# A decoder layer on one core: the attention stage takes rows transposed by the host, GpSimd adds the exponentials of the two key tiles, and the query halves are summed in turn

## The chip, the cores and the metric

The kernel runs on one core of a Trainium2 chip. The metric is the device time of one execution in microseconds; 687.07 us is the median of three runs (686.49 to 687.9).

## What is computed

One layer of a decoder on x of 8 batches x 256 rows x 512: attention, a long convolution against a context, and a feed-forward block with ternary weights. The change touches the attention alone:

```python
def rmsnorm(x):
    return x * jax.lax.rsqrt(jnp.mean(x * x, axis=-1, keepdims=True) + EPS)
x_ = _layernorm(x, axis=-1)
Q = (x_ @ Wq).reshape(B, T, HQ, Dh).transpose(0, 2, 1, 3)     # B 8, T 256, HQ 16, Dh 32
V = (x_ @ Wv).reshape(B, T, HKV, Dh).transpose(0, 2, 1, 3)    # HKV 4
Q = rmsnorm(Q)
K = rmsnorm(V)
scores = jnp.einsum('bhgtd,bhsd->bhgts', Q.reshape(B, HKV, g, T, Dh), K)
p = jax.nn.softmax(scores, axis=-1)                           # the mask is empty
y = jnp.einsum('bhgts,bhsd->bhgtd', p, V)
x = x + rmsnorm(y @ Wo)
```

A layer norm of the new x follows, whose rows are the queries of the convolution.

## The kernel before

The program is a sequence of stages. The attention stage takes the batches one at a time: a **turn** i of 8 does the scores, exponentials, sums, values and output projection of batch i, and between them the projections Q and V of batch i+1, and the transposed rows (xn2) of batch i-1 for the convolution. Turns 1 to 5 are a loop, turns 0, 6 and 7 are written out; turn 0 makes no projections (batch 1's are made ahead of it) and turn 7 has no next batch. Every engine has its own list of instructions, written by hand in `turn` of its block, and runs it in that order; semaphores alone tie the engines together. So a wait in one list holds everything behind it on that engine.

In a turn TensorE (PE) makes 16 scores tiles (`scores(i, n)`, L246): key head kv (of 4), key tile s (of 2, 128 keys each) and query half gp (of 2, 512 columns each). They go alternately to the two PSUM banks SB, ScalarE (ACT) takes each by `exponential` (L396) into `pt`, and score n waits for exponential n-2. Between the scores stand `x_transpose` (L205, the normalised rows of batch i+1, copied out by ACT's `x_out`, L360), `v` (L211) and `q` (L217). Then `sum_weights` (L264) multiplies all of `pt` by ones for the softmax sums, `q2_transpose` (L254) turns the rows of batch i-1, `sum_values` (L273) makes p V, `qk_transpose` (L229, L233) turns Q and K of the next batch, and `project` (L284) multiplies by Wo. A matmul in f32 shows as two records in the trace.

VectorE (DVE) has `rows_in` (statistics and normalised rows of batch i+2), `qk_norms` (the root of the mean squares of batch i+1 by Newton steps), `q_normalise` (L528), for each query half a reciprocal of the sums (L550) and a product (L555), `q_low` (L543: the low parts of Q), and `residual` (L560 on). After `q_low`, the SyncE queue (SP) issues 16 DMAs that spread Q over the partitions (`spread_q`, L158: 4 to each key head, semaphores d_qx0 to d_qx3). ACT also sums the feed-forward weights (`weight_sums`, L417: two tiles of 128x2048 in each turn). GpSimd (POOL) has only the powers of 128x2 variances (L639) and a copy of V (L646).

These lines set the order of the scores and what they wait for, before:

```python
def score(n):
    return n // 4, n // 2 % 2, n % 2        # kv, s, gp
...
if n % 4 == 0:
    wait(pe, d_qx[kv], i, 4 * 16)
...
if n >= 2:
    wait(pe, s_e, i, n - 1)
```

## Time and profile before

| | us |
|---|---|
| median of 3 runs | 687.07 |
| the profiled execution, its own time | 686.38 |
| its span in the trace | 684.6 |
| a turn of the loop, first score to first score | 32.3 |
| turns 1 to 6 together (63.20 to 256.87) | 193.67 |
| turn 0 (31.69 to 63.20) | 31.51 |
| turn 7 (256.87 to 286.66) | 29.79 |

The span is what the trace covers; the execution's own time is 1.8 us more. The attention stage ends with turn 7 at about 287 us; the convolution and the feed-forward block follow. Times in the rows below are microseconds from the start of the span unless marked ns.

### The profile page before, as it was taken

The numbers are of one execution on the slowest core, as the hardware profiler recorded it, in microseconds if no ns is written. First come the engines' busy times: TensorE is split into PE (matmuls) and PEld (weight loads), VectorE is DVE, ScalarE is ACT, GpSimd is POOL, SyncE is SP. The second block draws the span as 40 slices with busy tenths as digits, with TensorE's granted clock in tenths as the row PEclk, the third lists the DMA queues.
The fourth block names the chain that finished last, engine by engine and source line by source line (L and its number), as shares of the span: only waits on it lengthen the run. The fifth ranks groups of instructions, "written<-read, shape, count | busy, mean of one in ns | idle before, by whom it ended". The sixth has DMA issues, their size and how long they took to land.

```text
span 684.6 us, 10990 instructions
## 1 busy us (share of the span) xinstructions
PE 624.9 (91%) x3074; PEld 355.3 (52%) x3074; DVE 508.5 (74%) x981; ACT 455.5 (67%) x799; POOL 269.7 (39%) x248
## 2 busy tenths in 40 slices
PE   5889999999999998989999999948799999999995
PEld 3535454545454543467777777723344444444442
DVE  3556757575847373547887788789999999999983
ACT  2354666676665746168889888845876777577691
POOL 1000010001010003057777777624665666566572
PEclk9969999999999997999999999978999999999999
DMA  8564153627180816045666556511011100100001
GB/s 316 140 182 93 31 124 123 148 97 191 55 240 17 234 37 153 11 145 162 168 192 173 173 164 193 156 70 31 17 32 48 45 31 31 61 31 31 31 17 46
DMA packets 42309, 72.51 MB, mean 106 GB/s; under 512 B 4720, under 2 KB 16496, under 8 KB 42160
## 3 DMA queue, kind: packets, MB, share of 16 engines
q1 hardware_dynamic: 42288, 72.26, 36.7%
q8 instruction: 10, 0.16, 0.1%
q14 instruction: 11, 0.09, 0.0%
HBM read 47.51 MB, written 4.28 MB: 76 GB/s over the span
## 4 chain that ended last, share of the span: by engine, by line
PE 26%; DVE 24%; issue 5%; DVEq 1%; ACT 1%; POOL 0%; ACTq 0%; POOLq 0%
PE ps L708 20%; DVE toep L1189 4%; DVE xq L1175 3%; PE ps L1066 3%; DVE mb L1193 3%; DVE act8t L1225 2%; PE ps L1054 2%; DVE mx L1160 1%; DVE x_all L1138 1%; DVE st L1143 1%; DVE xn L1156 1%; DVE qo L761 1%; DVEq L69 1%; DVE ot L1233 1%; DVE cx L1171 0%
## 5 line engine op out<-in xcount | busy, mean ns | idle before, releaser
L708 PE MATMUL ps<-kv,toep 128*128 128x288 f32 x640 | 157.1, 409 | 1.1 <-PEq L1378 1.1
L708 PEld LDWEIGHTS ps<-kv,toep 128*128 128x128 f32 x640 | 122.2, 191 | 36.0 <-issue 2.2
L1066 PE MATMUL ps<-wt,xqt 128*128 128x512 bf16 x512 | 123.8, 387 | 9.4 <-DVE toep L1189 8.5
L1318 POOL TENSOR_TENSOR big<-toep,wst 128x512 f32<-128x512 f32 x64 | 83.6, 1306 | 59.7 <-DVE toep L1189 59.7
L396 ACT ACTIVATE big<-ps,kscale 128x512 f32<-128x512 f32 x128 | 84.3, 695 | 14.1 <-PE ps L246 13.3
L246 PE MATMUL ps<-qx,kx 128*128 128x512 f32 x128 | 76.7, 634 | 12.4 <-ACT big L396 12.1
L1066 PEld LDWEIGHTS ps<-wt,xqt 128*128 128x128 bf16 x512 | 48.3, 99 | 67.1 <-DVE toep L1189 11.9
L761 DVE TENSOR_REDUCE qo<-big 128x2048 f32 (+1 forms) x32 | 72.2, 2257 | 0.0
L1104 ACT ACTIVATE asq<-toep 128x512 f32<-128x512 f32 x64 | 39.5, 618 | 44.7 <-DVE sm L1199 43.7
L696 POOL TENSOR_TENSOR kv<-ctx 128x768 f32<-128x768 f32 (+1 forms) x32 | 52.5, 1642 | 37.0 <-PE ps L708 28.2
L750 DVE TENSOR_TENSOR big<-ps,qd 128x1024 f32<-128x1024 f32 x32 | 39.2, 1225 | 37.0 <-ACT ys L840 34.4
L1054 PE MATMUL ps<-wt,act8t 128*128 128x512 bf16 x256 | 59.9, 379 | 7.3 <-DVE act8t L1225 7.3
L550 DVE RECIPROCAL yt<-ps 128x512 f32<-128x512 f32 x16 | 53.6, 3351 | 14.6 <-PE ps L264 14.6
L217 PE MATMUL ps<-wq_s,xt 128*128 128x512 f32 x128 | 63.3, 593 | 0.8 <-ACT xt L360 0.8
L800 POOL TENSOR_TENSOR big<-ys,qd 128x768 f32<-128x768 f32 x32 | 56.3, 1759 | 13.7 <-ACT ys L840 11.5
L284 PE MATMUL ps<-wo_s,yt 128*128 128x512 f32 x128 | 56.6, 594 | 1.0 <-DVE yt L555 1.0
L246 PEld LDWEIGHTS ps<-qx,kx 128*128 128x128 f32 x128 | 25.7, 205 | 46.4 <-ACT big L396 26.6
L646 POOL COPY vo<-vn 128x256 f32<-128x256 f32 x8 | 3.2, 397 | 111.7 <-PE ps L273 86.3
L1189 DVE TENSOR_TENSOR toep<-ps,kv 128x512 f32<-128x512 f32 x64 | 43.5, 680 | 3.8 <-ACT kv L1095 2.4
L1054 PEld LDWEIGHTS ps<-wt,act8t 128*128 128x128 bf16 x256 | 23.9, 98 | 40.4 <-DVE act8t L1225 11.0
L1093 ACT ACTIVATE kv<-ps 128x512 f32<-128x512 f32 x64 | 37.6, 587 | 10.6 <-PE ps L1066 10.6
L1193 DVE TENSOR_REDUCE mb<-big 128x1 f32<-128x512 f32 x64 | 43.3, 677 | 0.0
(121 smaller groups left out, 1018.5 us busy)
## 6 DMA issues: line engine op xcount, KB each, us to landing
qx<-kv SPq DMA_DIRECT2D x128, 128.0 KB, 2.4
wst<-in_wall SPq DMA_DIRECT2D x12, 1024.0 KB, 6.8
wst<-in_wall SPq DMA_DIRECT2D x48, 256.0 KB, 3.8
toep<-krows SPq DMA_DIRECT2D x32, 256.0 KB, 3.7
ctx<-in_ctxt SPq DMA_DIRECT2D x32, 192.0 KB, 2.6
out_y<-ot SPq DMA_DIRECT2D x16, 256.0 KB, 2.0
conv_part<-qo SPq DMA_DIRECT2D x14, 256.0 KB, 2.7
x_all<-in_x SPq DMA_DIRECT2D x2, 1536.0 KB, 14.4
```

The source lines that it names most:

```text
L217: mm = pe.matmul(bank[:, t, :], xt[:, k, t * P:(t + 1) * P], wq_s[:, k, :], start=(k == 0), stop=(k == CK - 1))
L246: pe.matmul(SB[:, n % 2, :], kx[:, kv, s * P:(s + 1) * P].bitcast(F32R), qx[:, kv, gp * C:(gp + 1) * C].bitcast(F32R), start=True, stop=Tr ...
L284: mm = pe.matmul(OB[:, t, :], yt[:, k, t * P:(t + 1) * P], wo_s[:, k, :], start=(k == 0), stop=(k == CK - 1))
L396: act.activation(pt[:, s, kv, gp * C:(gp + 1) * C], SB[:, n % 2, :], ACT.Exp, scale=kscale[:, c:c + 1]).then_inc(s_e.sem, 1)
L708: mm = pe.matmul(m.ps[:, LB * r + lb, :].rearrange("p (b s) -> p b s", s=WIDE)[:, :, 0:PAIRS], m.toep[r][:, d * P:(d + 1) * P], m.kv[r][:, ...
L761: nc.vector.tensor_reduce(qo[:, :, bass.ds(h * HD, HD)], z[r][:], AX.X, ALU.add).then_inc(s_red.sem, 1)
L800: nc.gpsimd.tensor_tensor(z[r][:, :, :, HD - SHIFTS:HD].rearrange("p n j s -> p n s j"), window(ys[r][:], SHIFTS - 1, (SHIFTS * EW, NB), ( ...
L1054: mm = pe.matmul(DB, act8t[:, k, :], down_w[:, k, :], start=(k == 0), stop=(k == FK - 1))
L1066: mm = pe.matmul(bank[:, n % 2, :], xqt[r][:, k, :], wt[:, k, n * C:(n + 1) * C], start=(k == 0), stop=(k == CK - 1))
L1189: nc.vector.tensor_tensor(a[n % 2][:], UB[:, n % 2, :], r2[n % 2][:], ALU.mult).then_inc(s_a.sem, 1)
L1193: nc.vector.tensor_reduce(mb4[:, n:n + 1], act_w[r][:, n * C:(n + 1) * C], AX.X, ALU.max, apply_absolute_value=True).then_inc(s_mb4.sem, 1)
L1318: nc.gpsimd.tensor_tensor(act_w[r][:, n * C:(n + 1) * C], a[n % 2][:], gb[:, n * C:(n + 1) * C], ALU.mult).then_inc(s_w.sem, 1)
```

## The change

Every part is in the attention stage.

- The host also hands in x transposed (`xt`, per batch 128 x 4 x 256). PE multiplies it with Wq and Wv directly. Layer norm's mean is taken out of the weights: at the start PE sums the columns of Wv and Wq (`column_sums`) and DVE subtracts the mean (`centre`). The row's factor 1/sigma cancels in Q and K, except that epsilon is multiplied by the variance (`ev1`); V gets it in GpSimd's `values`, which is now a multiplication. `x_transpose`, `x_out` and the writing of `xn` are gone. A DMA of 512 KB for each batch loads the rows (`next_rows`).
- GpSimd adds the exponentials of the two key tiles (`add_weights`, 8 additions of 128x512 in a turn), and the softmax sums then take half as many matmuls.
- Scores run over all key heads for query half 0, then for half 1. `v` stands ahead of the scores. The sums of half 0 stand between scores 10 to 15; the projection takes half 0 of its depth first.
- ACT's `weight_sums` comes ahead of `q2_out`; DVE's `q_normalise` ahead of the first reciprocal; GpSimd does the powers `ro` and `rs4` of a batch in the next turn, among its additions.

```diff
+    value_bank, weight_bank = (OB[:, 0, :], SB[:, 1, :]), (OB[:, 1, :], SB[:, 0, :])
...
-        return n // 4, n // 2 % 2, n % 2
+        return n // 2 % HKV, n % 2, n // (2 * HKV)
...
+        def next_rows(i):
+            wait(sp, s_q, i, 2)
+            sp.dma_start(xt_s, xt[bass.ds(i + 1, 1)].rearrange("o p k t -> (o p) k t")).then_inc(d_xt.sem, 16)
...
-        sp.dma_start(x_all[:, 0], x_in[:, 0]).then_inc(d_x0.sem, 16)
         sp.dma_start(wv_s[:], wv.rearrange("(k p) n -> p k n", p=P)).then_inc(d_wv.sem, 16)
         sp.dma_start(wq_s[:], wq.rearrange("(k p) n -> p k n", p=P)).then_inc(d_wq.sem, 16)
+        sp.dma_start(xt_first, xt[0]).then_inc(d_xt0.sem, 16)
+        sp.dma_start(x_all[:, 0], x_in[:, 0]).then_inc(d_x0.sem, 16)
+        sp.dma_start(xt_s, xt[1]).then_inc(d_xt.sem, 16)
...
                          wall[r * 4:(r + 1) * 4].rearrange("b p n -> p b n")).then_inc(d_ws[r].sem, 16)
...
-        def x_transpose(i, t):
-            wait(pe, s_xn, i, t + 1)
+        def column_sums(bank, w, done):
             for k in range(CK):
-                mm = pe.transpose(TB[:, t, k * P:(k + 1) * P], xn[:, t, k * P:(k + 1) * P], m.ident[:])
-            mm.then_inc(s_xt.sem, 1)
-
-        def v(i, t):
-            wait(pe, s_xte, i, t + 1)
+                mm = pe.matmul(bank, m.ones[:], w[:, k, :], start=(k == 0), stop=(k == CK - 1))
+            mm.then_inc(done.sem, 1)
+
+        def v(i, t, rows=xt_s):
+            if t == 0 and rows is xt_s:
+                wait(pe, d_xt, i - 1, 16)
+                wait(pe, s_qhi, i - 1, 1)
+                wait(pe, s_qlo, i - 1, 1)
             for k in range(CK):
-                mm = pe.matmul(TB[:, 0, t * P:(t + 1) * P], xt[:, k, t * P:(t + 1) * P], wv_s[:, k, :],
+                mm = pe.matmul(TB[:, 0, t * P:(t + 1) * P], rows[:, k, t * P:(t + 1) * P], wv_s[:, k, :],
...
             kv, s, gp = score(n)
-            if n % 4 == 0:
+            if n < 2 * HKV and s == 0:
                 wait(pe, d_qx[kv], i, 4 * 16)
-            if n % 8 == 0:
-                wait(pe, s_kx, i, n // 8 + 1)
...
+        def sum_weights(i, gp, has_prev):
+            wait(pe, s_ps, i, HKV * (gp + 1))
+            if gp == 0 and has_prev:
+                wait(pe, s_x1, i - 1, 2)
+            for kv in range(HKV):
+                mm = pe.matmul(weight_bank[gp][kv * DH:(kv + 1) * DH, :], m.ones[:, 0:DH], pts[:, (gp * HKV + kv) % 6, :],
+                               start=True, stop=True)
+            mm.then_inc(s_den.sem, 1)
+
+        def sum_values(i, gp, s, has_prev):
+            if s == 0:
+                wait(pe, s_e, i, 2 * HKV * (gp + 1))
+            if s == 0 and gp == 0:
+                wait(pe, s_vo, i, 1)
+                if has_prev:
+                    wait(pe, s_x1, i - 1, 1)
+                else:
+                    wait(pe, s_qn, i + 1, 2)
+            for kv in range(HKV):
+                mm = pe.matmul(value_bank[gp][kv * DH:(kv + 1) * DH, :], vo[:, s, kv * DH:(kv + 1) * DH],
+                               pt[:, s, kv, gp * C:(gp + 1) * C], start=(s == 0), stop=(s == TT - 1))
+            if s == TT - 1:
                 mm.then_inc(s_pv.sem, 1)
...
+                        mm = pe.matmul(OB[:, t, :], yt[:, k, t * P:(t + 1) * P], wo_s[:, k, :],
+                                       start=(k == 0), stop=(k == CK - 1))
+                    if gp == 1:
+                        mm.then_inc(s_wo.sem, 1)
 
         def turn(i, has_prev=True, has_next=True):
             makes_next = has_prev and has_next
+            if makes_next:
+                for t in range(TT):
+                    v(i + 1, t)
             scores(i, 0)
             scores(i, 1)
-            for t in range(TT):
-                if makes_next:
-                    x_transpose(i + 1, t)
-                scores(i, 2 + t)
-            for t in range(TT):
-                if makes_next:
-                    v(i + 1, t)
-                scores(i, 4 + t)
             for n in range(TT * CK):
                 if makes_next:
                     q(i + 1, n // CK, n % CK)
-                scores(i, 6 + n)
-            for t in range(TT):
-                scores(i, 14 + t)
-            sum_weights(i)
+                scores(i, 2 + n)
+            scores(i, 10)
+            sum_values(i, 0, 0, has_prev)
+            scores(i, 11)
+            sum_values(i, 0, 1, has_prev)
+            scores(i, 12)
+            scores(i, 13)
+            sum_weights(i, 0, has_prev)
+            scores(i, 14)
+            scores(i, 15)
+            for s in range(TT):
+                sum_values(i, 1, s, has_prev)
+            sum_weights(i, 1, has_prev)
             for t in range(TT):
                 if has_prev:
                     q2_transpose(i - 1, t, has_next)
...
 
-        pe.wait_ge(c_ident.sem, 2)
+        pe.wait_ge(c_ones.sem, 1)
+        pe.wait_ge(d_wv.sem, 16)
+        column_sums(SB[:, 1, 0:P], wv_s, c_wvsum)
+        pe.wait_ge(d_wq.sem, 16)
+        column_sums(SB[:, 0, :], wq_s, c_wqsum)
+        pe.wait_ge(d_xt0.sem, 16)
+        pe.wait_ge(c_wv.sem, 1)
         for t in range(TT):
-            x_transpose(0, t)
-        pe.wait_ge(d_wv.sem, 16)
...
             makes_next = has_prev and has_next
-            exponential(i, 0)
-            exponential(i, 1)
-            for t in range(TT):
-                if makes_next:
-                    x_out(i + 1, t)
-                exponential(i, 2 + t)
-            exponential(i, 4)
             if makes_next:
+                wait(act, s_sso, i - 1, 2)
                 v_out(i + 1)
-            for n in range(5, 10):
+            for n in range(6):
                 exponential(i, n)
             if makes_next:
                 q_square(i + 1, 0)
-            for n in range(10, 13):
+            for n in range(6, 10):
                 exponential(i, n)
             if makes_next:
                 q_square(i + 1, 1)
-            for n in range(13, 16):
+            for n in range(10, 16):
                 exponential(i, n)
+            if has_next and has_prev:
+                weight_sums(i)
             for t in range(TT):
                 if has_prev:
                     q2_out(i - 1, t)
             if has_next:
-                if has_prev:
-                    weight_sums(i)
                 qk_out(i + 1)
             project(i, has_prev)
 
...
+        def rows_var(i, first=False):
+            if not first:
+                wait(dve, s_rs1, i - 1, 1)
             layer_norm_stats(i, stats, mv, ve1, s_bn1, s_mv1, s_ve1)
-            wait(dve, s_rs1, i, 1)
-            for t in range(TT):
...
 
-        def turn(i, has_prev=True, has_next=True, rows=True):
+        def turn(i, has_prev=True, has_next=True):
             if has_next:
                 k_low(i + 1)
-                if rows:
-                    rows_in(i + 2)
+                rows_var(i + 1)
                 qk_norms(i + 1)
-                if not has_prev:
-                    q_normalise(i + 1, bank=OB)
+                q_normalise(i + 1, bank=MB if has_prev else OB)
             else:
                 weight_sums()
-            invert_sums(i, 0)
-            if has_next:
-                if has_prev:
-                    q_normalise(i + 1)
-                k_scales(i + 1)
-            outputs(i, 0)
-            invert_sums(i, 1)
-            outputs(i, 1)
+            for gp in range(2):
+                invert_sums(i, gp)
...
+        def add_weights(i, n, has_prev):
+            gp, kv = n // HKV, n % HKV
+            wait(pool, s_e, i, 2 * (n + 1))
+            if n == 6:
+                wait(pool, s_den, i, 1)
+            elif n == 0 and has_prev:
+                wait(pool, s_den, i - 1, 2)
+            nc.gpsimd.tensor_tensor(pts[:, n % 6, :], pt[:, 0, kv, gp * C:(gp + 1) * C],
+                                    pt[:, 1, kv, gp * C:(gp + 1) * C], ALU.add).then_inc(s_ps.sem, 1)
+
+        def turn(i, has_prev=True, has_next=True):
+            if has_prev:
+                power(ro, ve3, s_ve3, s_ro, i - 1)
+            for n in range(2):
+                add_weights(i, n, has_prev)
+            if has_prev:
+                power(rs4, ve4, s_ve4, s_rs4, i - 1)
+            for n in range(2, 2 * HKV):
+                add_weights(i, n, has_prev)
             if has_next:
+                power(rs1, ve1, s_ve1, s_rs1, i + 1)
                 values(i + 1)
-            power(ro, ve3, s_ve3, s_ro, i)
```

The order of PE's instructions at the end of the scores of turn 6, before (`big` is the exponentials `pt`, `ones` gives sums of weights, `vo` values, `xn` the rows for the convolution):

```order
L246 MATMUL ps<-qx,kx 128x512 [waits s_e] x3
L264 MATMUL ps<-big,ones 32x512 [waits s_e]
L264 MATMUL ps<-big,ones 32x512 x7
L264 MATMUL ps<-big,ones 32x512 [waits s_e]
L264 MATMUL ps<-big,ones 32x512 x7
L254 MATMUL ps<-ident,xn 128x128 [waits s_klo,s_xn2]
L254 MATMUL ps<-ident,xn 128x128 x3
L254 MATMUL ps<-ident,xn 128x128 [waits s_klo,s_xn2]
L254 MATMUL ps<-ident,xn 128x128 x3
L273 MATMUL ps<-big,vo 32x512 [waits s_vo]
L273 MATMUL ps<-big,vo 32x512 x15
```

and now (`pts` is what GpSimd added; four values sums, then four weights sums at the end):

```order
L292 MATMUL ps<-big,vo 32x512 [waits s_x1,s_vo,s_e]
L292 MATMUL ps<-big,vo 32x512 x3
L262 MATMUL ps<-qx,kx 128x512 [waits s_e]
L292 MATMUL ps<-big,vo 32x512 x4
L262 MATMUL ps<-qx,kx 128x512 [waits s_e] x2
L278 MATMUL ps<-pts,ones 32x512 [waits s_x1,s_ps]
L278 MATMUL ps<-pts,ones 32x512 x3
L262 MATMUL ps<-qx,kx 128x512 [waits s_e] x2
L292 MATMUL ps<-big,vo 32x512 [waits s_e]
L292 MATMUL ps<-big,vo 32x512 x7
L278 MATMUL ps<-pts,ones 32x512 [waits s_ps]
L278 MATMUL ps<-pts,ones 32x512 x3
```

Eight matmuls of values and four of weights now stand among the scores; eight and four stay behind the last one, where 16 and 16 stood.

The scores of turn 7 on PE, before (d_qx0 to d_qx3 are the DMAs of key heads 0 to 3):

```order
L246 MATMUL ps<-qx,kx 128x512 [waits s_kx,d_qx0]
L246 MATMUL ps<-qx,kx 128x512
L246 MATMUL ps<-qx,kx 128x512 [waits s_e] x2
L246 MATMUL ps<-qx,kx 128x512 [waits s_e,d_qx1]
L246 MATMUL ps<-qx,kx 128x512 [waits s_e] x3
L246 MATMUL ps<-qx,kx 128x512 [waits s_e,s_kx,d_qx2]
L246 MATMUL ps<-qx,kx 128x512 [waits s_e] x3
L246 MATMUL ps<-qx,kx 128x512 [waits s_e,d_qx3]
L246 MATMUL ps<-qx,kx 128x512 [waits s_e] x3
```

and now:

```order
L262 MATMUL ps<-qx,kx 128x512 [waits s_kx,d_qx0]
L262 MATMUL ps<-qx,kx 128x512
L262 MATMUL ps<-qx,kx 128x512 [waits s_e,d_qx1]
L262 MATMUL ps<-qx,kx 128x512 [waits s_e]
L262 MATMUL ps<-qx,kx 128x512 [waits s_e,s_kx,d_qx2]
L262 MATMUL ps<-qx,kx 128x512 [waits s_e]
L262 MATMUL ps<-qx,kx 128x512 [waits s_e,d_qx3]
L262 MATMUL ps<-qx,kx 128x512 [waits s_e] x4
```

The last group of DMAs is asked for at score 6 where it was at score 12, that of head 2 at score 4 where it was at 8, and that of head 1 at 2 where it was at 4.

GpSimd's instructions from turn 6 on, before (`kv<-ctx` is the convolution's first work):

```order
L646 COPY vo<-vn 128x256 [waits s_vn,s_pv]
L639 TENSOR_TENSOR ro<-ve,half 128x2 [waits s_ve3]
L639 TENSOR_TENSOR rs<-ve,half 128x2 [waits s_ve4]
L696 TENSOR_TENSOR kv<-ctx 128x32x4x8 [waits d_ctx0,s_sc]
L701 TENSOR_TENSOR kv<-ctx 128x32x4
```

and now, turn 6 alone:

```order
L644 TENSOR_TENSOR ro<-ve,half 128x2 [waits s_ve3]
L661 TENSOR_TENSOR pts<-big 128x512 [waits s_den,s_e]
L661 TENSOR_TENSOR pts<-big 128x512 [waits s_e]
L644 TENSOR_TENSOR rs<-ve,half 128x2 [waits s_ve4]
L661 TENSOR_TENSOR pts<-big 128x512 [waits s_e] x4
L661 TENSOR_TENSOR pts<-big 128x512 [waits s_den,s_e]
L661 TENSOR_TENSOR pts<-big 128x512 [waits s_e]
L644 TENSOR_TENSOR rs<-ve,half 128x2 [waits s_ve1]
L652 TENSOR_TENSOR vo<-vn,rs 128x256 [waits s_rs1,s_vn,s_pv]
```

The power `rs` behind s_ve4, which DVE needs for the rows of batch i-1, now stands behind two additions that wait for exponentials of turn i.

## Rows read from the trace of the kernel before

**Rows 1.** Stages: length, busy PE, PEld, DVE, ACT, POOL, clock, DMA share, GB/s.

```profile
63.20:95.53 32.33, 31.19 (x161) 16.01 (x161) 21.67 (x41) 21.32 (x37) 2.47 (x4) 1.00 0.30 66
256.87:286.66 29.79, 26.23 (x107) 10.02 (x107) 12.82 (x18) 12.53 (x22) 6.10 (x6) 0.83 0.37 93
31.69:63.20 31.51, 27.35 (x114) 10.97 (x113) 17.65 (x31) 14.90 (x27) 1.09 (x2) 0.78 0.51 137
```

**Rows 2.** Timeline of turn 1, which begins at 63.20: start, length, engine, line, instructions.

```profile
68.00 0.38 ACT L366 ACTIVATE sq<-ps 128x256 f32<-128x256 f32 x1
...
69.01 2.09 ACT L396 ACTIVATE big<-ps,kscale 128x512 f32<-128x512 f32 x3
...
70.22 1.02 PE L217 MATMUL ps<-wq_s,xt 128*128 128x512 f32 x2
...
71.31 1.02 PE L217 MATMUL ps<-wq_s,xt 128*128 128x512 f32 x2
...
76.74 0.60 ACT L376 ACTIVATE sq<-ps 128x512 f32<-128x512 f32 x1 [0.17 <-PE ps L217]
77.23 1.96 ACT L396 ACTIVATE big<-ps,kscale 128x512 f32<-128x512 f32 x3
...
78.55 3.64 PE L264 MATMUL ps<-big,ones 128*32 128x512 f32 x32
...
80.75 3.35 DVE L550 RECIPROCAL yt<-ps 128x512 f32<-128x512 f32 x1
...
82.12 1.09 PE L254 MATMUL ps<-ident,xn 128*128 128x128 f32 x8
82.90 1.07 ACT L401 COPY qo<-ps 128x512 f32 x2 [3.71 <-PE ps L254]
...
83.86 1.92 ACT L417 ACTIVATE wst<-wst 128x2048 f32<-128x2048 f32 x1
84.01 1.22 DVE L528 TENSOR_TENSOR qn<-ps,rqk 128x512 f32<-128x512 f32 x2
...
85.82 3.35 DVE L550 RECIPROCAL yt<-ps 128x512 f32<-128x512 f32 x1
...
86.71 1.09 PE L229 MATMUL ps<-ident,qn 128*128 128x128 f32 x8
...
88.52 7.03 PE L284 MATMUL ps<-wo_s,yt 128*128 128x512 f32 x16
...
89.28 0.69 DVE L555 TENSOR_TENSOR yt<-ps,yt 128x512 f32<-128x512 f32 x1
...
89.89 1.28 DVE L543 TENSOR_TENSOR kv<-ps,kv 128x512 fp32r<-128x512 f32 x2
```

**Rows 3.** SP's queue in turn 1: the DMAs that spread Q.

```profile
91.24 10.04 SPq L158 DMA_DIRECT2D qx<-kv  x16
```

**Rows 4.** The same DMAs over all turns: issue to landing.

```profile
DMA to landing us min/median/max: 2.3/2.4/3.5
```

**Rows 5.** GpSimd's two-input operation on 128x512 in the feed-forward block.

```profile
L1318 POOL TENSOR_TENSOR big<-toep,wst x64: 1284/1301/1465, 462.7 to 666.6; 128x512 f32<-128x512 f32 x64
```

**Rows 6.** Timeline of the start and turn 0.

```profile
9.49 3.14 PE L211 MATMUL ps<-wv_s,xt 128*128 128x128 f32 x16
...
12.47 7.03 PE L217 MATMUL ps<-wq_s,xt 128*128 128x512 f32 x16
...
27.32 11.03 SPq L158 DMA_DIRECT2D qx<-kv  x16
...
29.87 1.95 PE L211 MATMUL ps<-wv_s,xt 128*128 128x128 f32 x16
...
45.56 5.51 PE L264 MATMUL ps<-big,ones 128*32 128x512 f32 x32 [0.20 <-ACT big L396]
```

**Rows 7.** Timeline of turn 7, which begins at 256.87.

```profile
262.53 1.34 PE L246 MATMUL ps<-qx,kx 128*128 128x512 f32 x2 [0.23 <-ACT big L396]
...
268.85 4.80 PE L264 MATMUL ps<-big,ones 128*32 128x512 f32 x32 [0.20 <-ACT big L396]
```

More of the change, by code:

```diff
@@ L484, in layer_norm_stats, with centre @@
             nc.vector.tensor_scalar(ve[:], mv[:, :, 1], LN_EPS, None, ALU.add).then_inc(var.sem, 1)
-        def rows_in(i, first=False):
+        def rows_var(i, first=False):
+            if not first:
+                wait(dve, s_rs1, i - 1, 1)
             layer_norm_stats(i, stats, mv, ve1, s_bn1, s_mv1, s_ve1)
-            wait(dve, s_rs1, i, 1)
-            for t in range(TT):
-                if not first:
-                    wait(dve, s_xt, i - 1, t + 1)
-                nc.vector.tensor_scalar(xn[:, t, :], row(i, t), mv[:, t, 0:1], rs1[:, t:t + 1],
-                                        ALU.subtract, ALU.mult).then_inc(s_xn.sem, 1)
+            nc.vector.tensor_scalar(ev1[:], mv[:, :, 1], LN_EPS, RMS_EPS, ALU.add, ALU.mult).then_inc(s_ev1.sem, 1)
+        def centre(w, sums, summed, done):
+            dve.wait_ge(summed.sem, 1)
+            nc.vector.scalar_tensor_tensor(w, sums, -1.0 / C, w, ALU.mult, ALU.add).then_inc(done.sem, 1)
         def k_low(i):
@@ L629, in _ @@
         turn(0, has_prev=False)
+        dve.wait_ge(d_x.sem, TT * 16)
         with dve.Fori(1, B - 2) as i:
             turn(i)
-        turn(B - 2, rows=False)
+        turn(B - 2)
         turn(B - 1, has_next=False)
@@ L662, in _ @@
         values(0, first=True)
-        power(rs1, ve1, s_ve1, s_rs1, 1)
-        turn(0)
+        turn(0, has_prev=False)
         with pool.Fori(1, B - 2) as i:
             turn(i)
-        turn(B - 2, rows=False)
+        turn(B - 2)
+        turn(B - 1, has_next=False)
         wait(pool, s_sc, B - 1, 16)
@@ L672, in _ @@
             context_products(nc, m, r, 0).then_inc(m.s_kv.sem, 1)
-        turn(B - 1, has_next=False, rows=False)
+        power(ro, ve3, s_ve3, s_ro, B - 1)
+        power(rs4, ve4, s_ve4, s_rs4, B - 1)
 def load_toeplitz(eng, m, krows, h, r):
```

131 lines of the change are left out of this document (55 added, 76 removed).

## Prediction

> **What bounds the kernel now.** I first read the table of stages [rows 1]. Turn 1 takes 32.33 us and PE is busy for 31.19 of them at the full clock (1.00, the 2.4 GHz level), DVE for 21.7, ACT for 21.3, GpSimd for 2.5. So a turn of the loop is PE's own list of instructions. Turns 0 and 7 differ: PE is granted 0.78 and 0.83 there, because it waits between scores. Then I read the timeline of turn 1 for the price of each piece on PE [rows 2]. A Q matmul and a score together take 1.09 us (70.22 to 71.31). An f32 matmul of 512 columns is two records of 0.44 (7.03 for 16), some 0.85, so a score costs 0.24. The sums of weights occupy PE for 3.57 us (78.55 to 82.12), the transposes for the convolution and the values sums for 4.59 (82.12 to 86.71), about 1.0 and 3.57. The transposes of Q and K take 1.8 (86.71 to 88.52), the projection 6.9 (88.52 to the next turn's start at 95.53 is 7.0, with some 0.1 of waiting). Eight V matmuls take 1.95 [rows 6]. The last exponential ends at 79.19, that is 16.0 after the turn began.
>
> Last I followed Q from DVE to PE. `q_low` ends at 91.17 and SP starts its 16 DMAs at 91.24 [rows 2, 3]. They are issued in 10.04 us, 0.63 each, and land 2.4 after issue [rows 3, 4]. The groups of four are therefore in at 4.35, 6.9, 9.4 and 11.9 us after `q_low`. The first was in at 95.5, just when the turn began at 95.53; the fourth was in at 103, and score 12 came later.
>
> **What a turn loses.** Eight transposes go, about 1.0 us. The sums of weights are halved: 1.8 gone. Counted in work, PE needs v 1.95, scores 3.84, Q 6.8, values 3.57, weights 1.8, transposes 1.0 and 1.8, projection 6.9: 27.7 us. What it waits for decides the rest, so I lay the new turn out from its start at 0 with the prices above.
>
> - `v` 0 to 2.0; scores 0 and 1 end at 2.5. But `v_out` now stands ahead of exponential 0 on ACT. It held ACT for 1.01 us before (68.00 to 69.01), so exponential 0 ends at about 3.9 and score 2, behind Q matmul 0, waits from 3.3 to 4.0: 0.7 lost. From there pairs of 1.09; score 9 ends at 11.9.
> - Exponential 9 runs 12.1 to 12.8, then `q_square` takes 0.5 of ACT (76.74 to 77.23), and six more exponentials at 0.65 (1.96 for three). With 0.9 us sums between the scores, scores 12 to 15 come a little late; I put the last exponential's end at 17.7.
> - Values of half 1 then 17.7 to 19.6. GpSimd's last addition starts at 17.8. I take 1.30 us for it [rows 5]; it ends at 19.1, under the values. Weights of half 1 to 20.5, the row transposes to 21.5.
> - `weight_sums` now holds ACT from 17.7 for 3.9 (two of 1.92 and their reads), so `q2_out` runs 21.6 to 22.7 [rows 2]. `qk_transpose` writes the banks that it empties, so it starts at 22.2, and without `weight_sums` it would be 22.0: the order costs little, but nothing covers this copy any more, where the values sums did. 0.7 lost. It ends at 24.1.
> - DVE: from the end of `q_square` (77.34) to the end of the Newton steps (80.75) 3.4, so `q_normalise` is at 16.9 to 18.1. First reciprocal and product to 22.2 (85.82 to 89.28 is 3.46, plus 0.6). The second pair to 26.3, `q_low` to 27.5. The projection needs the first product at 24.1 and has it, and the second at 27.5 and has it. It ends at 31.0.
>
> So **a turn is about 31.1 us**, 1.2 less, not the 2.8 of work removed: the score part is longer by its sums and only partly hides them. The same number comes from the other loop. Score 6 at 8.4 leads to `q_square`'s end at 13.3, `q_low`'s end at 27.5, and the fourth group of DMAs 11.9 later, at 39.4, needed by score 6 of the next turn at 8.4 + 31.1 = 39.5. It is that tight because the new score order wants the groups at scores 0, 2, 4, 6. Any delay on DVE's chain would go straight into the turn. Six turns: 193.67 before, 186.6 after, **-7.1**.
>
> DVE's residual of batch i-1 gets its second power behind two additions, some 2.5 us later than before, at 8.3. `q_low`'s chain starts at 13.3, and the residual, `k_low` and the statistics are done near 12. This is hidden with about 1 us to spare. The GpSimd total is 8 x 1.3 + 3 powers + V, about 13 of 31 us; each pair of exponentials comes 2.2 apart in the loop, so it keeps up. The DMA of 512 KB has 20 us; DMA share was 0.30 to 0.51 in these stages [rows 1]. Both cost nothing.
>
> **The start.** Before, Q's matmuls of batch 0 ended at 19.5 [rows 6]. Now PE needs both weights, sums their columns, and waits for `centre` in its first step. I have no row for when Wq lands if it goes second; before it was not needed until 12.47. Bounds: 6 us (the Q matmuls can't start before it) to 12. I take 8.5. The column sums are 8 records of 512: 3.5 us at full clock. The 16 V records took 3.14 early against 1.95 warm, so up to 5.7. I take 5. V 2, Q 7.0: end at 22.9, **+3.4** (bounds +0.5 to +6).
>
> **Turn 0.** Here scores are paced by exponentials, two in 1.6 us. SP takes 11.03 for 16 DMAs, 0.69 each [rows 6]. From `q_low` the groups land at 4.5, 7.3, 10.0 and 12.8, that is 0, 2.8, 5.6 and 8.4 after the first score. Scores 4 and 6 would want theirs at about 4.4 and 6.0, so 2.5 is lost. The sums among scores cost 1 to 2 more, since the exponentials do not cover a slower PE. Behind the last score, 5.5 + 3.6 us of sums become 2.7, and 3.46 + 0.6 of the second reciprocal and product follow. The projection's first half runs beside them. The end comes at 30.5 instead of 31.5: **-1** (bounds -4 and +2).
>
> **Turn 7.** The fourth group lands at 27.5 + 11.9 - 31.1 = 8.3 after its start; score 6 was at 262.53, 5.7 in [rows 7]. With the 1 to 2 us for sums inside, the last exponential ends 4 to 6 us later than its 12.5. Behind it 4.80 + 1.0 + 3.6 of sums and transposes [rows 7] become 2.7 + 1.1, and one of two reciprocals is hidden: 5 to 6 saved. **0** (bounds -4 and +2). The convolution's first products on GpSimd take 5 us from there (6.10 busy in this stage), and the projection needs longer, so they are hidden.
>
> **Sum.** -7.1 + 3.4 - 1 + 0 = -4.7 on a span of 684.6, own time 686.38: 681.7. The median of the runs is 0.7 higher, so 682.4; I say 682.
>
> **Does GpSimd pay?** The addition is 1301 ns in a stage where DVE is busy, at least 1284, at most 1465 [rows 5]. With 1.3 the last addition has 0.4 us in hand under the values. The Trainium skill (GPSIMD Engine Reference, Engine selection) tells you not to put two-input elementwise work on GpSimd, about 2x slower than VectorE; the rows agree roughly, since DVE's product of this size takes 0.69. By that rule the eight additions belong on DVE. There they would cost 5.5 us of its chain, so the trace speaks for this place. The same page (Specifications) says that GpSimd shares SBUF interfaces with VectorE and that DVE instructions with two SBUF inputs contend.
>
> **Rivals.**
> 1. *Gains at both ends.* Wq lands by 7, the sums run at full clock, and turns 0 and 7 save 3 each: 682.4 - 2 - 2 - 3 = 675. For it: the reciprocals dominate their ends. Against: the DMA groups. Chance 0.18.
> 2. *DVE is stretched by GpSimd.* The additions run all through the Newton steps, whose operands are in SBUF. The largest over the smallest in [rows 5] is 14%, which on the 4 us of reduce and Newton steps is 0.6 a turn, 3.6 in all: 686, no change. Chance 0.15.
> 3. *Slower: DVE's chain waits for whole additions.* If two DVE steps in the chain (the row normalisation and one Newton step) each wait out an addition of 1.3, the chain grows by up to 2.6 less the 1 in hand, and as SP's 16 DMAs hang on it, so does the turn: 32.7. Six turns then cost +2.5 where I have -7.1: 692. It decides from 1.2 us a turn on. Against: DVE and GpSimd run side by side in the feed-forward block, with additions stretched by 14% at most. With a bad start (Wq at 12, +6) less stretching is enough. Chance 0.17.
>
> My forecast (678.5 to 685.7) has 0.5. Range 674.5 to 689.5. Two runs of this kernel are told apart from 0.2%, 1.4 us. Faster by more than that: the forecast and rival 1, 0.68. Within it: 0.15. Slower: 0.17.
>
> **What would show it.** A turn in the loop of 31.1 us by the table of stages; the first score of a turn 2 us after the first V matmul; score 2 waiting 0.7 for ACT; `qk_transpose` waiting for `q2_out`; SP's fourth group landing within 0.5 us of score 6; the first score of turn 0 near 35; additions of 1.3 us. I am wrong if score 6 waits long for its DMAs in the loop (rival 3), if Newton steps are over 0.2 us each (rival 2), or if the first score comes before 33 (rival 1).

## The result, and the profile after

The changed kernel takes 705.09 us (median of 4 runs, 704.46 to 707.93), the kernel before 686.78 us beside it on the same chip. The ratio is 1.0276, 95% interval 1.0251 to 1.0301: slower, where I had forecast 682 us.

The table of stages of the changed kernel (columns as in [rows 1]): turn 0 from its first score, turn 3 of the loop, and turn 7 from the end of the projection before it.

```profile
33.68:64.55 30.87, 23.91 (x100) 9.57 (x98) 18.84 (x30) 15.00 (x27) 11.51 (x10) 0.83 0.52 148
132.83:167.24 34.41, 30.19 (x137) 14.16 (x136) 25.56 (x40) 20.65 (x35) 13.18 (x12) 1.00 0.49 137
270.71:302.53 31.82, 23.81 (x91) 9.06 (x91) 14.00 (x18) 12.69 (x22) 16.22 (x14) 0.79 0.40 99
```

A turn of the loop is 34.41 us, not 31.1. PE is busy for 30.19 of them, so it waits for 4.2, at the full clock. Turns 1 to 6 take 206.16 us (64.55 to 270.71) against 193.67. The span, 703.6 us, is 19.0 longer:

| part | predicted | measured |
|---|---|---|
| start, to the first score of turn 0 | +3.4 | +2.0 (33.68 against 31.69) |
| turn 0 | -1 | -0.6 |
| turns 1 to 6 | -7.1 | +12.5 |
| turn 7 | 0 | +2.0 |
| all behind it | 0 | +3.1 |

Of the last row, 2.7 us is one group of matmuls near the end, in this profiled execution (last section).

What PE waits for between 70 and 290 us (total us, times, longest), after:

```profile
PE ps L262 <- DMA qx<-kv: 12.4, 12, 1.8
PE ps L304 <- DVE yt L565: 7.8, 12, 1.0
PE ps L292 <- ACT big L413: 6.7, 6, 1.1
PE ps L245 <- ACT qo L418: 3.2, 6, 0.5
```

Before, the same view has three rows: exponentials 8.0, a product 1.0, exponentials again 0.2. Of the 12.4 us for the DMAs of Q, 6.3 stand in turn 7 (see its bullet below); the other 6.0 and the 7.8 for the products stand in the loop. Both wait for VectorE's chain: the DMAs start behind `q_low`, and the projection needs the products. So I went to DVE's timeline in turn 3, with GpSimd's additions (L661) and one of its powers (L644) among its steps:

```profile
147.08 1.28 POOL L661 TENSOR_TENSOR pts<-big 128x512 f32<-128x512 f32 x1 [0.91 <-ACT big L413]
147.52 0.82 DVE L514 TENSOR_REDUCE ssq<-sq 128x20 f32<-128x640 f32 x1 [0.54 <-ACT sq L394]
148.61 0.18 DVE L522 TENSOR_SCALAR nt<-ve 128x40 int32<-128x40 int32 x1
148.73 1.28 POOL L661 TENSOR_TENSOR pts<-big 128x512 f32<-128x512 f32 x1 [0.37 <-ACT big L413]
148.83 1.23 DVE L525 TENSOR_SCALAR rqk<-nt 128x40 int32<-128x40 int32 x1
150.09 0.20 DVE L529 TENSOR_TENSOR nt<-rqk 128x40 f32<-128x40 f32 x1
...
150.82 1.29 POOL L661 TENSOR_TENSOR pts<-big 128x512 f32<-128x512 f32 x1 [0.81 <-ACT big L413]
151.02 1.15 DVE L531 SCALAR_TENSOR_TENSOR nt<-nt,ve 128x40 f32<-128x40 f32 x1
152.21 0.20 DVE L533 SCALAR_TENSOR_TENSOR rqk<-nt,rqk 128x40 f32<-128x40 f32 x1
152.39 1.29 POOL L661 TENSOR_TENSOR pts<-big 128x512 f32<-128x512 f32 x1 [0.28 <-ACT big L413]
152.44 1.30 DVE L529 TENSOR_TENSOR nt<-rqk 128x40 f32<-128x40 f32 x1
153.64 0.70 POOL L644 TENSOR_TENSOR rs<-ve,half 128x2 f32<-128x2 f32 x1
153.78 0.20 DVE L531 SCALAR_TENSOR_TENSOR nt<-nt,ve 128x40 f32<-128x40 f32 x1
```

Each Newton step that begins just behind an addition's start ends with that addition (148.83 + 1.23 = 150.06; the addition ends at 150.01), and the steps between additions take 0.20 us. Three of the ten are held, by 1.05, 0.95 and 1.10 us: 3.1 us. It is the same in each of turns 1 to 6, three of the ten and 3.1 us. The wait hides in the duration; the view lists no idle time for it. The reduce that begins inside the addition of 147.08 takes its usual 0.82. The last two steps (153.78 and 154.01) begin inside a GpSimd instruction too, the power of 153.64, and keep their 0.20.

The steps over all turns (min, median, max in ns), first before, then after:

```profile
L519 DVE TENSOR_TENSOR nt<-rqk x24: 199/200/202, 21.5 to 241.6; 128x40 f32<-128x40 f32 x24
L515 DVE TENSOR_SCALAR rqk<-nt x8: 183/185/185, 21.3 to 239.9; 128x40 int32<-128x40 int32 x8
```

```profile
L529 DVE TENSOR_TENSOR nt<-rqk x24: 199/201/1298, 23.7 to 255.9; 128x40 f32<-128x40 f32 x24
L525 DVE TENSOR_SCALAR rqk<-nt x8: 184/1228/1228, 23.5 to 252.1; 128x40 int32<-128x40 int32 x8
```

**The row that I had not looked for.** The trace of before shows the same thing in the feed-forward block, where I had found "additions stretched by 14% at most". I had looked at GpSimd's durations [rows 5], and the engine that is held is DVE. By line, before:

```profile
L1175 DVE TENSOR_SCALAR xq<-xn,s x16: 478/1670/1686, 455.8 to 646.0; 128x512 f32<-128x512 f32 x16
L1193 DVE TENSOR_REDUCE mb<-big x64: 674/677/681, 468.9 to 668.7; 128x1 f32<-128x512 f32 x64
L1164 DVE TENSOR_SCALAR cl<-mx x16: 153/154/155, 455.1 to 644.8; 128x1 f32<-128x1 f32 x16
```

A step that can take 0.478 us takes 1.67 in the median, held by 1.2 us behind a GpSimd instruction (at 512.53 it begins 0.5 us into one of 1.89), while the reductions never leave 0.68, although 56 of the 64 begin inside one of GpSimd's additions. Steps on a single column are not held either: 15 of the 16 of L1164 begin inside an addition and all take 0.15. The Trainium skill (SBUF — State Buffer, "Who interferes with whom") states it as a rule: VectorE and GpSimd share one pair of SBUF ports, "it's an exclusive lock", held for a whole instruction, and it names two-input operations from SBUF and `tensor_scalar` among those that can contend and `tensor_reduce` among those that never do. This trace agrees for the additions and for the GpSimd step beside L1175: the held steps are of the first two kinds, with 0.95 to 1.2 us each, and L1193 is of the third. It does not show the hold for GpSimd's power on 128x2: in each of turns 1 to 6 of the changed kernel two two-input Newton steps begin inside it and keep their 0.20 us. Whether its reads were over by then can't be told from the profile.

### The profile page after: what moved, and what is told of

It reads as the page before. It is cut to its first block, busy times and chain, and to the rows that moved or that the text cites. A ratio compares the mean times of both kernels' runs of the same rounds, so it can differ in the third digit from the quotient of the medians.

```text
span 703.6 us, 10776 instructions
## 1 busy us (share of the span) xinstructions
PE 619.9 (88%) x2898; PEld 342.4 (49%) x2898; DVE 534.5 (76%) x978; ACT 449.5 (64%) x783; POOL 354.3 (50%) x312
## 4 chain that ended last, share of the span: by engine, by line
PE 25%; DVE 23%; issue 5%; DVEq 1%; DMA 1%; ACT 1%; POOL 0%; SPq 0%; ACTq 0%; POOLq 0%
PE ps L730 19%; DVE toep L1211 4%; DVE xq L1197 3%; PE ps L1088 3%; DVE mb L1215 3%; PE ps L1076 2%; DVE act8t L1247 2%; DVE mx L1182 1%; DVE x_all L1160 1%; DVE st L1165 1%; DVE xn L1178 1%; DVE qo L783 1%; DMA toep<-krows 1%; DVEq L69 1%; DVE ot L1255 1%
## 5 line engine op out<-in xcount | busy, mean ns | idle before, releaser
L661 POOL TENSOR_TENSOR pts<-big 128x512 f32<-128x512 f32 x64 | 83.2, 1301 | 82.1 <-ACT big L413 82.0
L262 PE MATMUL ps<-qx,kx 128*128 128x512 f32 x128 | 67.7, 578 | 20.1 <-DMA qx<-kv 15.2
L1076 PE MATMUL ps<-wt,act8t 128*128 128x512 bf16 x256 | 62.6, 392 | 7.3 <-DVE act8t L1247 7.3
L718 POOL TENSOR_TENSOR kv<-ctx 128x768 f32<-128x768 f32 (+1 forms) x32 | 52.7, 1647 | 30.6 <-PE ps L730 27.8
L304 PE MATMUL ps<-wo_s,yt 128*128 128x512 f32 x128 | 58.6, 603 | 7.8 <-DVE yt L565 7.8
L233 PE MATMUL ps<-wq_s,qo 128*128 128x512 f32 x128 | 63.0, 592 | 0.0
L262 PEld LDWEIGHTS ps<-qx,kx 128*128 128x128 f32 x128 | 24.2, 204 | 75.1 <-ACT big L413 44.3
L644 POOL TENSOR_TENSOR ro<-ve,half 128x2 f32<-128x2 f32 x8 | 5.5, 692 | 95.4 <-DVE ve L570 95.4
L428 ACT ACTIVATE sq<-ps 128x512 f32<-128x512 f32 x16 | 9.6, 597 | 55.1 <-PE ps L304 55.1
```

The source lines that it names most:

```text
L233: mm = pe.matmul(bank[:, t, :], rows[:, k, t * P:(t + 1) * P], wq_s[:, k, :], start=(k == 0), stop=(k == CK - 1))
L262: pe.matmul(SB[:, n % 2, :], kx[:, kv, s * P:(s + 1) * P].bitcast(F32R), qx[:, kv, gp * C:(gp + 1) * C].bitcast(F32R), start=True, stop=Tr ...
L304: mm = pe.matmul(OB[:, t, :], yt[:, k, t * P:(t + 1) * P], wo_s[:, k, :], start=(k == 0), stop=(k == CK - 1))
L661: nc.gpsimd.tensor_tensor(pts[:, n % 6, :], pt[:, 0, kv, gp * C:(gp + 1) * C], pt[:, 1, kv, gp * C:(gp + 1) * C], ALU.add).then_inc(s_ps.s ...
L1076: mm = pe.matmul(DB, act8t[:, k, :], down_w[:, k, :], start=(k == 0), stop=(k == FK - 1))
```

## The experiments

Theory A: DVE is held by additions in progress, and its chain is on the path. Theory B: the change loses elsewhere (score order, rows by DMA, PE's list), or GpSimd's additions cost by their own lateness.

**1. No additions.** The sums read key tile 0 only.

```diff
-            for n in range(2):
-                add_weights(i, n, has_prev)
...
-                mm = pe.matmul(weight_bank[gp][kv * DH:(kv + 1) * DH, :], m.ones[:, 0:DH], pts[:, (gp * HKV + kv) % 6, :],
+                mm = pe.matmul(weight_bank[gp][kv * DH:(kv + 1) * DH, :], m.ones[:, 0:DH],
+                               pt[:, 0, kv, gp * C:(gp + 1) * C], start=True, stop=True)
```

> The changed kernel (705.1 us, 34.4 a turn of the loop) without GpSimd's additions; the sums of weights take the exponentials of key tile 0 directly, so PE has the same list of matmuls, and the other half of each softmax sum is left out of the result. Theory A (DVE instructions that read through the second SBUF interface wait for a whole addition, three times 1.05 us a turn between q_square and q_low): Newton steps all back at 0.20, a turn of 31.1 to 31.5, the DMA waits gone with them, about 686. Theory B (the new score order asks for the DMAs of Q too soon, and that sets the turn, additions or not): the turn stays over 33.5 and the time over 700.

Measured: 686.75 us, ratio 0.9976 (0.9948 to 1.0003), turn 31.35 us, all Newton steps at 0.20. As A had it: without GpSimd's work everything else of the change gives the forecast turn.

**2. The kernel before, with the additions.** Eight additions a turn into a tile that nobody reads, each behind its pair of exponentials.

```diff
+                wait(pool, s_e, i, 2 * (n + 1))
...
+                nc.gpsimd.tensor_tensor(added[:], wq_s[:, 0, :], wq_s[:, 1, :], ALU.add).then_inc(s_add.sem, 1)
```

> The kernel before (686.8 us, 32.3 a turn) with eight additions of 128x512 on GpSimd in turns 0 to 6, behind the same exponentials as in the changed kernel, into a tile that nobody reads. Theory A: several Newton steps take 1.0 to 1.3 us instead of 0.20 and q_low comes 1 to 3 us later; its first DMAs landed just in time before, so a turn becomes 33.3 to 35.4 and the time 693 to 705. Theory B: no more than 1 us in all, 687.

Measured: 707.31 us, ratio 1.0277 (1.0231 to 1.0323), turn 35.5. Both lie just above what I gave for theory A. Nobody reads what these additions write, and they cost 20.6 us. But the held steps are mostly others than in the changed kernel. Its Newton steps:

```profile
L521 DVE TENSOR_TENSOR nt<-rqk x24: 199/199/1296, 21.9 to 260.9; 128x40 f32<-128x40 f32 x24
L517 DVE TENSOR_SCALAR rqk<-nt x8: 184/1142/1168, 21.7 to 258.3; 128x40 int32<-128x40 int32 x8
```

and the normalisation of rows in turns 1 to 5, before and here:

```profile
L492 DVE TENSOR_SCALAR xn<-x_all,mv,rs x10: 540/545/547, 73.3 to 203.0; 128x512 f32 x10
L494 DVE TENSOR_SCALAR xn<-x_all,mv,rs x10: 1366/1436/1503, 76.5 to 219.8; 128x512 f32 x10
```

I expected several held Newton steps, and in turns 1 to 5 one of the ten is held (L517, by 0.96 us), with the step that makes their input (L511, by 0.86). The other 3.7 us of a turn are in four normalisations of rows like those above. Those come ahead of the second reduce, where the kernel before waits 2.1 us for the squares, so 1.6 of the 3.7 count. 1.6 + 0.86 + 0.96 is 3.4 us, and the turn is 3.2 longer. The hold is theory A's; the place of most of it is the row normalisation that rival 3 names.

**3. The transposed rows and centred weights alone**, with the order of scores and sums of before.

```diff
-        return n // 2 % HKV, n % 2, n // (2 * HKV)
+        return n // 4, n // 2 % 2, n % 2
```

> Only the first part of the change: rows transposed by the host, weights centred, x_transpose and x_out gone; score order, sums, projection and ACT's and DVE's order as before, v one place earlier. PE has 1.0 us less a turn, the start is 2.0 later. Theory A: no addition, no slow Newton step, a turn of 31.3 to 31.8, about 684 (681 to 687). Theory B has the same for the turn, as the score order is the old one. A third theory (the transposed rows themselves cost, by their DMA or their 1 KB pieces) would give over 690.

A miss: 691.07 us, ratio 1.0056 (1.0029 to 1.0082), turn 31.83. Eight transposes go and the turn gets 0.45 shorter, not 1.0: PE waits 0.54 and 0.57 for exponentials at the end of the score part instead. The start costs 1.5 (first score at 33.15), and in the profiled execution turn 6 took 33.4, with a granted clock of 0.51 from 239.1 to 242.6.

**4. No additions, all sixteen products of the sums on PE.** Experiment 1 with both key tiles summed.

```diff
+            for s in range(TT):
+                for kv in range(HKV):
+                    mm = pe.matmul(weight_bank[gp][kv * DH:(kv + 1) * DH, :], m.ones[:, 0:DH],
+                                   pt[:, s, kv, gp * C:(gp + 1) * C], start=(s == 0), stop=(s == TT - 1))
```

> The changed kernel without additions, with the sums of weights over both key tiles on PE (16 matmuls a turn instead of 8), everything else as changed; a complete result. Theory A: Newton steps at 0.20; PE has 1.8 us more than in e1, so a turn of 32.5 to 33.0, and 694 (690 to 698). Theory B: over 700.

Measured: 694.84 us, ratio 1.0119 (1.0066 to 1.0172), turn 32.63. Both are inside what theory A gave. Against experiment 1 (31.35), the second eight products cost 1.3 us a turn. So the additions do save PE 1.3 us a turn, and cost DVE 3.1.

**5. The additions in halves.**

```diff
+            for h in range(2):
+                lo, hi = gp * C + h * C // 2, gp * C + (h + 1) * C // 2
```

> The changed kernel with each of GpSimd's additions written as two instructions of 256 columns instead of one of 512. Theory A (a VectorE instruction that reads two tiles of SBUF, or copies with a scalar from SBUF to SBUF, is held until the GpSimd instruction in progress ends): a held step waits for at most about 0.65 us instead of 1.1 us, so the longest `nt` step falls from 1298 ns to about 0.75 to 0.9 us; some more steps are held than before because there are twice as many ends to be caught between. The turn goes from 34.45 us to 33 to 34 us, the time from 705 to 694 to 703 us. Theory B (the two engines share the interface by bytes, so that what counts is how much both read in a stretch): the held steps add up to the same, the turn stays at 34.3 to 34.9 us and the time at 704 to 709 us. Longest `nt` step under 1.0 us is A, at 1.2 us is neither.

Measured: 701.71 us, ratio 1.0189 (1.0156 to 1.0223), turn 34.15, just above the range I gave. The longest `nt` step is 0.76 us, as A had it: a hold ends with the GpSimd instruction. But more steps are held, six of the ten in each of turns 1 to 6, by 0.42 to 0.49 us, so 2.8 us a turn remain of 3.1. The means between 70 and 290 us:

```profile
L533 DVE SCALAR_TENSOR_TENSOR rqk<-nt,rqk 128x40 f32<-128x40 f32 x18 | 9.0, 503 | 0.6
L531 DVE SCALAR_TENSOR_TENSOR nt<-nt,ve 128x40 f32<-128x40 f32 x18 | 8.9, 496 | 0.6
L529 DVE TENSOR_TENSOR nt<-rqk 128x40 f32<-128x40 f32 x18 | 6.4, 356 | 0.6
```

**6. Head 1's copies of Q from ScalarE's queue.**

```diff
+            wait(act, s_qlo, i, 2)
+            for row in range(4):
+                act.dma_start(qx[row * DH:(row + 1) * DH, 1, :], qpart[row % 2][DH:2 * DH, :]).then_inc(d_qx[1].sem, 16)
```

> The changed kernel with the four copies of head 1 of Q issued from ScalarE's DMA queue instead of SyncE's (ScalarE issues them right behind its copies of Q and K; it is otherwise idle there). It changes nothing of VectorE and GpSimd. Theory A says that the held VectorE steps are about 3.1 us of what separates the turn of 34.45 us from the predicted 31.1 us, and that the late copies of Q, for which TensorE waits, carry them round the loop. If those copies add a cost of their own (TensorE waits for head 1 to 3 one after the other for 1.13 us at the front of its score part), the turn falls by 0.8 to 1.2 us, to about 33.3 us, and the time to 696 to 699 us. If the copies only hand on the lateness of q_low and bring nothing themselves, the turn stays within 0.3 us of 34.45 us and the time at 703 to 706 us.

A miss, and a badly chosen edit: 715.32 us, ratio 1.0387 (1.0357 to 1.0417), turn 36.84. Both expectations overlooked what stands behind the wait for `q_low` in ScalarE's list, the squares of the projection's output. In its timeline:

```profile
140.85 0.60 ACT L434 ACTIVATE sq<-ps 128x512 f32<-128x512 f32 x1 [9.46 <-issue]
```

They start 1.7 us after the next turn began (139.19), and ScalarE goes to the exponentials late. It tells nothing about the copies themselves.

**7. One power instead of ten Newton steps.**

```diff
+            nc.gpsimd.tensor_tensor(rqk[:], ve2[:], spread(half[:], NH), ALU.pow).then_inc(s_nr.sem, 1)
```

> The changed kernel with VectorE's ten Newton steps on the 128x40 variances replaced by one power instruction of GpSimd, put between two of its additions; all sixteen products of the sums stay. Theory A: the held steps were mostly these short ones on 128x40 (about 2.3 us of held time in a turn between L525 and L531) and they are on the path from the squares to q_low, so the turn falls by 2.5 to 3.4 us, to 31.1 to 32 us, and the time to 682 to 690 us, although the additions run as before. Theory B (the additions cost the turn in another way: writes that collide with the copies of Q, or GpSimd's additions late for the sums): the turn stays above 33 us and the time above 695 us.

A miss on its price: 735.91 us, ratio 1.0683 (1.0643 to 1.0722), turn 37.65. I had not bounded the instruction; one of 128x2 takes 0.70, this one of 128x40 takes 6.75:

```profile
L642 POOL TENSOR_TENSOR rqk<-ve,half x8: 6749/6752/6753, 24.0 to 284.7; 128x40 f32<-128x40 f32 x8
```

It is 4.2 us longer than the free Newton steps (143.67 to 146.18 in experiment 9, 2.5) and delays the additions behind it. It decides nothing between A and B.

**8. Experiments 6 and 7 together**, and one of ScalarE's weight sums behind its copies for the transposed rows.

```diff
+                weight_sums(i, (0,))
             for t in range(TT):
                 if has_prev:
                     q2_out(i - 1, t)
+            if has_next:
+                if has_prev:
+                    weight_sums(i, (1,))
```

> The changed kernel with three edits: VectorE's ten Newton steps replaced by one power instruction of GpSimd between two additions, the four copies of head 1 of Q issued from ScalarE's DMA queue, and one of the two weight sums of ScalarE moved behind its copies for the output's transposes. Theory A: without the held steps the turn falls back to what TensorE's list of work takes, 30.6 to 31.2 us, and the time to 678 to 684 us, below the kernel before. Rival: with VectorE out of the way ScalarE's exponentials bound the score part (with the rows alone changed they already did, at 31.83 us a turn), and the turn is 31.3 to 31.9 us and the time 684 to 689 us, no faster than before.

Measured: 737.62 us, ratio 1.0728 (1.0688 to 1.0768), turns of 37.3 to 37.7. It carries the faults of both, and tells no more than they do.

**9. The additions pause during the Newton steps.** All work stays; one wait on GpSimd is new, and the second half's weights are summed a little later.

```diff
-            for n in range(2, 2 * HKV):
+            for n in range(2, 5):
+                add_weights(i, n, has_prev)
+            if has_next:
+                wait(pool, s_nr, i + 1, 11)
+            for n in range(5, 2 * HKV):
                 add_weights(i, n, has_prev)
...
-            sum_weights(i, 1, has_prev)
             for t in range(TT):
                 if has_prev:
                     q2_transpose(i - 1, t, has_next)
+            sum_weights(i, 1, has_prev)
```

> The changed kernel with all its additions, but GpSimd stops after the fifth of a turn until VectorE's ten Newton steps for the next element are done, and then makes the last three; the sums of the second half's weights stand behind the transposes of the row before in TensorE's order, where they are needed. The work of every engine is the same. Theory A (a VectorE instruction is held only while a GpSimd addition is in progress, and what that costs is the place on the path from the squares to q_low): the `nt` and `rqk` steps are at 0.18 to 0.20 us but for one that meets the fifth addition, the turn falls from 34.45 us to 31.4 to 32.3 us and the time to 686 to 692 us. Theory B (the additions cost by their number or bytes wherever they stand, or by their own lateness): the turn stays at 33.5 us or above and the time at 698 us or above.

Measured: 686.69 us, ratio 0.999 (0.9962 to 1.0019), turn 31.40. It takes 18.4 us off the changed kernel with the same instructions. Between 70 and 255 us PE no longer waits for the products, and only once for the DMAs of Q (1.3 us). Its steps on DVE between 70 and 290 us (busy us, mean ns):

```profile
L529 DVE TENSOR_TENSOR nt<-rqk 128x40 f32<-128x40 f32 x18 | 3.6, 200 | 0.6
L525 DVE TENSOR_SCALAR rqk<-nt 128x40 int32<-128x40 int32 x6 | 1.1, 184 | 0.2
```

and the additions around them in one turn of its timeline:

```profile
142.14 1.28 POOL L661 TENSOR_TENSOR pts<-big 128x512 f32<-128x512 f32 x1 [0.91 <-ACT big L413]
146.34 3.76 POOL L661 TENSOR_TENSOR pts<-big 128x512 f32<-128x512 f32 x3 [2.93 <-DVE rqk L533]
```

Between the second reduce's start and `q_normalise` lie 3.64 us (142.58 to 146.22); in the changed kernel 6.72 (147.52 to 154.24). The difference, 3.08, is the turn's (34.41 less 31.40 is 3.01).

**10. The pause, with PE's order left alone.**

```diff
+            if has_next:
+                wait(pool, s_nr, i + 1, 11)
```

> As the run before (GpSimd pauses between its fifth and sixth addition until the Newton steps are done), but TensorE's order is left as it is in the changed kernel, with the second half's sums of weights ahead of the transposes. The last addition ends about 22 us into the turn and TensorE wants it at 20.5 to 21 us, so it waits for GpSimd for 0.5 to 1.5 us: the turn is 31.8 to 33 us and the time 688 to 696 us, by theory A. If the pause moves the lateness from VectorE to the sums in full, the turn stays at 34 us and the time at 702 us or above.

Measured: 688.0 us, ratio 1.0012 (0.9989 to 1.0036), turn 31.9. PE waits 0.78 us a turn for GpSimd's last addition, and the turn is 0.5 longer than in experiment 9. Turn, wait and time are at the lower end of what I gave.

**11. The moved sums, without the pause.** The control.

```diff
-            sum_weights(i, 1, has_prev)
             for t in range(TT):
                 if has_prev:
                     q2_transpose(i - 1, t, has_next)
+            sum_weights(i, 1, has_prev)
```

> The control of the two: the changed kernel without any pause, with the second half's sums of weights behind the transposes of the row before. Theory A has no use for it, since TensorE does not wait for the sums: turn 34.2 to 34.7 us, time 703 to 707 us. If the order of the sums alone were to bring something, it is below 702 us.

Measured: 706.26 us, ratio 1.0262 (1.0221 to 1.0303), turn 34.4. It came as expected. The order of the sums alone brings nothing. With it left alone the pause brings 17.1 us (experiment 10), with it 18.4. Theory B is out.

**12. The pause, and ScalarE's copies of Q and K ahead of its second weight sum.**

```diff
+            if has_next:
+                qk_out(i + 1)
+                if has_prev:
+                    weight_sums(i, (1,))
```

> The run with the pause in the Newton steps (turn 31.4 us, 686.7 us) plus one edit in ScalarE's order: of its two sums over the uploaded weights, which take 1.9 us each, the second stands behind the copies of Q and K instead of ahead of them, so that the copies for which TensorE waits 0.40 us a turn come 2 us earlier. The turn then goes to 30.9 to 31.1 us, the length of TensorE's own list, and the time to 683 to 685.5 us, 0.2 to 0.5% below the kernel before. If the exponentials or the copies of Q by DMA set the turn instead, it stays at 31.3 to 31.5 us and the time at 686 to 688 us.

Measured: 687.43 us, ratio 0.999 (0.997 to 1.0011), turn 31.34. It is a miss for the 30.9 to 31.1, and came out as I gave for the other case. The wait for the copies is gone, and the DMA of Q takes its place. PE's waits of experiment 9 in turns 2 to 5 (99 to 224 us):

```profile
PE ps L292 <- ACT big L413: 4.5, 4, 1.1
PE ps L262 <- ACT big L413: 1.9, 4, 0.5
PE ps L245 <- ACT qo L418: 1.6, 4, 0.4
```

and of this one (100 to 225 us):

```profile
PE ps L292 <- ACT big L413: 4.5, 4, 1.1
PE ps L262 <- DMA qx<-kv: 2.7, 5, 0.6
```

So with PE's other waits shortened the turn stays at 31.35 us, and what PE waits for is the loop from DVE over SyncE's sixteen DMAs. That this loop is the bound is read from these waits; no run shortened it. No version here beats the kernel before.

## Why the prediction was wrong

- **The step that failed** is the one against rival 3: "DVE and GpSimd run side by side in the feed-forward block, with additions stretched by 14% at most". It measured the engine that does not wait. So DVE's 3.4 us from the squares to the end of the Newton steps was taken as free of GpSimd; in turn 3 it was 6.7 (147.5 to 154.2), and 3.6 in experiment 9. The term that it spoiled is the -7.1 us of turns 1 to 6, measured as +12.5. Experiment 9, which has no held Newton step there, gives -3.2: the holds are 15.7 of the 19.6 us between.
- **The mechanism was rival 3's**, with a chance of 0.17. I had also undersized it: two held steps, one of them among the row's own, of which 1 us was in hand, 32.7 us a turn. In the changed kernel three steps are held behind the squares, where nothing is in hand: 3.1 us. With 31.35 (experiment 1) that is 34.45, and 34.41 was measured. In turns 3 to 6 a fourth step, of the row's own, is held by some 1.0 to 1.1 us ahead of the second reduce. It is hidden, as I had it for such a step: that reduce still waits 0.5 us for the squares. The meeting is no chance one, since additions and squares both follow the exponentials: L525 is held in all six turns.
- **The coupling** was right: the chain's delay went into the turn in full, by SP's queue and the products, as "any delay on DVE's chain would go straight into the turn" has it. The wait stands elsewhere than I would have looked: in turn 2 it is 1.10 us at score 2 and 0.23 at score 6, and 1.3 at the projection.
- **The turn of 31.1** was nearly right but for the holds: 31.40, 31.35 and 31.34 in turns 2 to 5 of three kernels without them. In experiment 9 `q_square` ends 13.5 us into the turn (13.3 predicted), `q_low` at 27.8 (27.5), `qk_transpose` waits 0.40 for `q2_out`, and the additions take 1.28 in the median (1.26 to 1.47). The exponentials end at 18.3 for the 17.7 put down; what the 0.3 left is made of was not taken apart. But one turn stood for six: turn 1 took 32.6 and turn 6 32.0 there, and so 3.9 us of the -7.1 were missing even without holds. What makes these two longer was not tried.
- **The start** was oversized, +2.0 for +3.4: Wq is there at 6.9 us, not 8.5. Its column sums take 5.94 us, more than the 5 for both, and the terms listed add up to 22.5, not 22.9. In the other kernels with this start Q's matmuls of batch 0 end at 21.1 to 22.7 us, and the first score stands at 33.3 to 36.2, since it can also wait for the DMAs of Q (1.63 us in experiment 10). So part of the +2.0 is the luck of one execution.
- **Turn 0**: -0.6 for -1, inside its bounds. **Turn 7**: +2.0 for 0, at the edge of its bounds, and still +1.7 in experiment 9, so most of it is not the holds'. PE waits there 1.80, 1.83, 1.27 and 1.44 us for the four groups of DMAs; in experiment 9 0.54, 1.85, 1.73 and 1.43. The new order wants a head every two scores, and no Q matmuls stand between the scores. Experiment 3, with the order of before, has no such wait in its turn 7. But the turn does not follow from these waits alone: experiment 10 has three of them (1.85, 1.58 and 1.46), and its turn 7 takes 28.9 us to the convolution, less than the 29.8 of before. That difference was not taken apart. The waits of the changed kernel:

```profile
272.51 0.73 PE L262 MATMUL ps<-qx,kx 128*128 128x512 f32 x2 [1.80 <-DMA qx<-kv]
275.08 1.22 PE L262 MATMUL ps<-qx,kx 128*128 128x512 f32 x2 [1.83 <-DMA qx<-kv]
277.57 1.22 PE L262 MATMUL ps<-qx,kx 128*128 128x512 f32 x2 [1.27 <-DMA qx<-kv]
280.23 1.22 PE L262 MATMUL ps<-qx,kx 128*128 128x512 f32 x2 [1.44 <-DMA qx<-kv]
```

- **Even without the holds it would have been no gain.** Experiment 9 against before: start and turn 0 +1.8, turns 1 to 6 -3.2, turn 7 +1.7 to the convolution, +0.2 in sum. The loop gives 0.9 a turn in four of the six, and the longer turns 1 and 6, the start and turn 7 take it back.

## What to carry to other kernels

Before work goes to GpSimd, list the VectorE instructions that will run beside it, and look in the trace for a line of VectorE whose median is far above its minimum while GpSimd is busy: in these kernels a two-input step from SBUF, or a `tensor_scalar` on two columns or more, was held for the rest of a GpSimd addition, however short it was itself. A step that was hidden with time in hand costs only what exceeds that time (experiment 2). A chain of many small steps is the worst neighbour, and the remedy is cheap where GpSimd has slack: let it pause for that chain. And price every new instruction from a row of its own size.
